# GpSimd multiplies the mask into the fourth head group of each attention chunk, VectorE into the first three

## The reference, cut to what matters

```python
w = softmax(einsum('btc,fc->btf', x, w_lin).reshape(B, T, 16, 31))
kidx = s_idx - t_idx + 30                      # place of source s among the taps of token t
we = where((kidx >= 0) & (kidx < 31), take_along_axis(w, clip(kidx, 0, 30)), 0)
out = einsum('bhts,bhsr->bhtr', we, xh)        # 16 channels a head
x = x + layernorm(out)
```

## Time and profile before

| | |
|---|---|
| median of 3 runs | 1038.87 us (1035.18 to 1041.07) |
| the profiled execution | 1037.57 us, of which the span is 1035.8 us |
| busy over the span | PE 92%, PEld 80%, DVE 82%, ACT 53%, POOL 56% |
| products of half 0 (first `am` to last `residual`) | 93.6 to 196.2 us |
| products of half 1 | 272.9 to 377.3 us |

### The profile page before, as it was taken

The page is one execution under the profiler, slowest core; times in us unless marked ns, Lnnn a source line. Parts: engine busy times, 40 slices in busy tenths (PEclk is TensorE's granted clock), DMA queues, the critical chain, the costliest instruction groups (busy, mean ns, idle before and its releaser), DMA issues.

```text
span 1035.8 us, 26916 instructions
## 1 busy us (share of the span) xinstructions
PE 951.2 (92%) x9256; PEld 833.6 (80%) x9256; DVE 844.7 (82%) x2278; ACT 550.8 (53%) x1308; POOL 582.2 (56%) x843
## 2 busy tenths in 40 slices
PE   5997899899789976899999999999999999999994
PEld 4766788687678865788888899999999878788883
DVE  5887998789799868888886588888888678788886
ACT  4995354799434453333434555555555445454542
POOL 4441655622056540268884366666662688888874
PEclk9998999899999988999999999999999999999996
DMA  5532578843268851122232465555556656665653
GB/s 164 172 110 59 163 208 247 259 124 113 65 173 225 236 186 62 50 88 62 76 119 62 88 202 176 179 177 175 176 180 134 188 178 186 190 199 172 207 166 110
DMA packets 155811, 158.17 MB, mean 153 GB/s; under 512 B 52528, under 2 KB 135600, under 8 KB 155696
## 3 DMA queue, kind: packets, MB, share of 16 engines
q1 hardware_dynamic: 137648, 113.98, 35.7%
q0 software_dynamic: 13056, 35.67, 13.0%
q10 hardware_dynamic: 4992, 6.95, 2.2%
HBM read 91.90 MB, written 64.63 MB: 151 GB/s over the span
## 4 chain that ended last, share of the span: by engine, by line
PE 25%; POOL 17%; DVE 12%; issue 4%; ACT 2%; DMA 1%; POOLq 0%; DVEq 0%; SPq 0%; ACTq 0%
POOL cy L1380 14%; PE bank L1245 11%; PE bank L1261 5%; PE bank L788 3%; PE bank L1230 3%; DVE in_blk L1067 2%; POOL crstd L1389 2%; PE bank L804 2%; DVE in_blk L1066 2%; DVE hf L768 2%; DVE hl L774 2%; ACT hh L751 1%; PE bank L1254 1%; DVE el L1074 1%; POOL crstd L1387 1%
## 5 line engine op out<-in xcount | busy, mean ns | idle before, releaser
L843 POOL DMA_INDIRECT xg<-yn_scratch,ids x144 | 137.0, 951 | 94.2 <-PE bank L1230 65.3
L1380 POOL DMA_INDIRECT cy<-expert_rows,slots x128 | 143.4, 1120 | 56.4 <-issue 36.5
L751 ACT ACTIVATE hh<-hf 128x512 fp32r<-128x512 f32 x96 | 60.7, 633 | 202.9 <-DVE hf L768 202.9
L788 PE MATMUL bank<-yh,gh 128*128 128x512 f32 x352 | 141.0, 401 | 12.5 <-DVE hf L768 12.3
L667 PE MATMUL bank<-xbd,am 128*32 128x68 f32 x4096 | 138.3, 304 | 13.6 <-DMA xbd<-xn_scratch 7.9
L667 PEld LDWEIGHTS bank<-xbd,am 128*32 128x32 f32 x4096 | 123.0, 129 | 21.3 <-issue 10.4
L788 PE MATMUL bank<-yh,gl 128*128 128x512 f32 x352 | 140.1, 398 | 0.0
L788 PE MATMUL bank<-yl,gh 128*128 128x512 f32 x352 | 139.2, 395 | 0.0
L945 POOL TENSOR_SCALAR in_row<-col,row_f 128x128 bf16<-128x128 bf16 x128 | 96.6, 771 | 65.6 <-DVE row_f L1051 39.6
L804 PE MATMUL bank<-dh,hh 128*128 128x256 f32 x384 | 110.2, 292 | 11.8 <-DVE hl L774 8.0
L804 PE MATMUL bank<-dl,hh 128*128 128x256 f32 x384 | 106.5, 282 | 0.0
(11 more groups left out here) (184 smaller groups left out, 2684.2 us busy)
## 6 DMA issues: line engine op xcount, KB each, us to landing
expert_rows<-yo SPq DMA_DIRECT2D x144, 128.0 KB
xbd<-xn_scratch SPq DMA_DIRECT2D x128, 72.0 KB, 2.3
xt<-xp SPq DMA_DIRECT2D x32, 256.0 KB, 2.7
xn_scratch<-xn SPq DMA_DIRECT2D x64, 128.0 KB, 2.7
xr<-x SPq DMA_DIRECT2D x32, 256.0 KB, 3.6
x_scratch<-x SPq DMA_DIRECT2D x32, 256.0 KB, 3.8
yn_scratch<-yn SPq DMA_DIRECT2D x32, 256.0 KB, 3.7
ynt_scratch<-ynt SPq DMA_DIRECT2D x32, 256.0 KB, 4.4
```

The lines of the kernel that those rows point to most:

```text
L751: self.nc.scalar.activation(self.hh[0:f, g], self.hf[0:f, k], ACT.Copy).then_inc(self.s["hh_ok"], 1)
L788: ins = self.nc.tensor.matmul(self.pb[2 * k + half][:], w[:, c, col:col + P], y[:, n % 2, c, :], start=(j == 0), stop=(j == 5))
L843: return nc.gpsimd.indirect_dma_start(out=to, out_offset=None, in_=yn_d.rearrange("n p c -> (n p) c"), in_offset=bass.IndirectOffsetOnAxis ...
L1380: nc.gpsimd.indirect_dma_start(out=y[:, r, t, j], out_offset=None, in_=yg_d, in_offset=bass.IndirectOffsetOnAxis(ap=slots[:, 2 * unit + t, ...
```

## The change

The fourth product of each chunk (group 3) moves from VectorE to GpSimd, as `masked_last`. In GpSimd's list of step i it stands behind `scales23(i-1)` and makes group 3 of chunk i+1. It has its own semaphore `am3_ok`; TensorE waits for that ahead of group 3 of each half, and ScalarE's `keep` waits for both at the start of the second half. Shapes, operands and values stay as they are.

```diff
+            def masked_last(n):
+                h, i, q = n // NCH, n % NCH, n % 2
+                if i == 0:
+                    po.wait_ge(s["probs_ok"], (h + 1) * J)
+                po.wait_ge(s["pso_full"], n + 1)
+                nc.gpsimd.tensor_tensor(
+                    am[:, q, NG - 1], probs[:, bass.ds(i * CB, CB), NG - 1, None, :].to_broadcast([P, CB, 2, J]),
+                    mask[:, None].to_broadcast([P, CB, 2, J]), ALU.mult).then_inc(s["am3_ok"], 1)
...
                 if 0 <= i - 1 < NCH + 2:
                     scales23(h, i - 1)
+                at(h, i + 1, masked_last)
...
                 ve.wait_ge(s["pso_full"], n + 1)
-                for g in range(NG):
+                for g in range(NG - 1):
                     nc.vector.tensor_tensor(
...
                 if n == NPR:
-                    act.wait_ge(s["am_ok"], NCH * NG)
+                    act.wait_ge(s["am_ok"], NCH * (NG - 1))
+                    act.wait_ge(s["am3_ok"], NCH)
...
                 for g in range(NG):
-                    pe.wait_ge(s["am_ok"], n * NG + g + 1)
+                    if g < NG - 1:
+                        pe.wait_ge(s["am_ok"], n * (NG - 1) + g + 1)
+                    else:
+                        pe.wait_ge(s["am3_ok"], n + 1)
```

More of the change, by code:

```diff
@@ L214, in attention @@
             psx_full xth_ok xtl_ok psl_full mx_ok sub_ok exp_ok pse_full probs_ok
-            xs_in0 xs_in1 am_ok pso_full rs_ok av_ok st2_ok mv2_ok var2_ok dev2_ok norm2_ok
+            xs_in0 xs_in1 am_ok am3_ok pso_full rs_ok av_ok st2_ok mv2_ok var2_ok dev2_ok norm2_ok
             z_ok xr_in0 xr_in1 x2_ok st3_ok mv3_ok yn_ok psy_full ynt_ok psg_full lg_ok
```

## The result

The changed kernel takes 1058.37 us (median of 4 runs, 1056.34 to 1060.02), the kernel before beside it 1039.97 us: ratio 1.0172, 95% interval 1.0146 to 1.0198. It is 18 us slower. The forecast had the direction, its range held the time, but the 9 us that it forecast are half of what came.

What follows compares the result with a forecast made beforehand. The prediction took the ring of GpSimd and ScalarE, 5.80 us a step, as the bound. Steps 6, ramps 4, less 1 back gave +9 us on 1037.57, 1046.6; with 1.3 to the median 1047.9, forecast 1048 us, 80% range 1040 to 1060.

Steps and rivals of the forecast that it cites:

- The ring through GpSimd and ScalarE: Steady steps: residual, scales23 (L361), centred and normal2 wait on each other without gaps and set the step of 5.80 us.
- Rival (d): Steady steps: VectorE is the bound and is relieved, 14.6 us less, 1024 us; chance under 1%, counted with (b).
- (a): Steady steps: TensorE's 1.6 us wait fits into its slack, hidden, no change, 1041 us; chance 21%.
- (b): Steady steps: VectorE's products slip behind L361, which falls from 0.55 to 0.20 us; faster, 1032 us; chance 6%.
- GpSimd's product: Behind L361 in GpSimd's list: the moved product takes 1.29 us, between 0.61 and 2.58, and fits into 2.34 us idle.
- Rival (c): GpSimd's product: repeated operands make it 2.58 us, 23 us in the steps and 6 for ramps, 1067 us; chance 18%.
- lighter form: Of the dear-product rival: half of its loss, or the stores of yn joining the loop, about 1057 us; no separate chance.
- the router loop: Late group 3 delays TensorE, router, put_logits and centred, then the product three chunks on: 0.6 us in two chunks, 0.3 each.
- 0.25 us a chunk, bounds 0.05 and 0.7: Steady steps: the loss taken for TensorE's wait for group 3, over 24 chunks 6 us (1 to 17).
- second loop: Late TensorE delays VectorE's group; GpSimd's product takes the port, moments up to 1.2 us late against 0.4 of slack.
- The ramps: First chunks of each half: later products cost 2 us for each ramp (0.7 to 4), so 4 us.
- What comes back: Places where the ring loses time to transfers: a slower pipeline leaves these more time, 1 us back in all.

## Why the prediction was wrong in size

*What bounds the kernel: right.* The ring through GpSimd and ScalarE sets 5.80 us; without any fourth product it stays 5.80, and with L361 free of the port it is 5.63. Rival (d), VectorE as the bound, fell with the run that leaves the product out: 5 us where it asked for about 15. Rivals (a), no change, and (b), faster, fell with the measured time and with TensorE's wait.

*GpSimd's product: right,* 1.25 to 1.30 us by itself, in an idle place of its list. Rival (c), a dear product, fell too. Its lighter form named 1057 us, close to the measured 1058, but for causes that the trace doesn't have: the product isn't dear, and ScalarE's waits name a store of yn once in both halves, for 2.0 us in half 1. It is also by this form that the range reached up to 1060.

*TensorE waits and the router loop: the mechanism right, and its 12.2 us right to 0.1,* as the run with the third product behind the moments shows. TensorE's wait was to be over 1 us in most steps; it is 0.97 us in one step and 0.27 in the next.

*The step that failed is the term "0.25 us a chunk, bounds 0.05 and 0.7".* The forecast named a second loop, in which TensorE's lateness delays VectorE's group and the port then makes the moments late, and counted it among "other waits can add"; for the sum it took less than even the router loop's 0.3, on the ground that products sliding behind L361 give time back. That second loop sets the pace. Read from the timeline above it closes: from the end of one L379 to TensorE's end of the chunk 3.4 us, VectorE's group 3.0, division and moments 2.4, `scales23` 2.2, the next L379 1.7, together 12.7 us for two chunks. An undisturbed step is 0.54 us longer, inside the bounds and twice the value taken. Over the 22 steps from chunk 2 to 13 the loss is 8.9 us, 0.40 a step, where 6 less 1 were forecast. Opening that loop in three ways (another order on TensorE, a third buffer, another order on VectorE) brought the undisturbed step from 6.34 us to 5.79, 5.82 and 6.10: all, all and about half of the 0.54.

*The ramps: mis-sized,* 3.6 us each instead of 2, as the run with the ramps on VectorE shows. The forecast's own bound of 0.7 to 4 us held it. Group 3 of chunk 2 was as late as worked out (it ends at 107.8, forecast 107.7), but what this starts was left out: the same second loop, with VectorE's group of 4.02 us. With TensorE's order changed a ramp cost 1.8 us, near the 2 of the forecast.

*What comes back: open.* Before, four steps from chunk 2 to 13 were over 5.80 us by 0.1 us or more, by 3.9 us together (6.65 in half 0; 5.95, 7.64 and 6.83 in half 1); after, one is longer than the others, 7.97 against 6.34, by 1.6 us. That is 2 us back where 1 was allowed. But such steps also vary by this much among the kernels with a step of 5.80 us (2 to 4 us together), so no run shows it apart.

*Of what the profile was to show:* the group of 32, the waits of TensorE and the longer step came; VectorE's busy time did not fall by 20 us, because its waits for the port are part of its instructions, and the rest of the program kept its length within its scatter.

## What to carry to other kernels

Before moving work to an idle engine, find when the consumer wants the result and what the new owner does ahead of it: here the work fitted into idle time, and TensorE still waited 0.97 us for it in every second step, because it stood behind a chain that VectorE's list hadn't had ahead of it. Then close every loop that the late result starts, over as many chunks as there are buffers, and let the longest one set the step; naming the second loop as a remark and taking a value below the first is how much of the loss was missed, in the steps and in the ramps. Work that reads SBUF on GpSimd should not be placed where a late VectorE can slide onto it.

## What the runs showed of the hardware

Repeated operands cost GpSimd nothing: 1.25 us for the 128x512 product against 1.29 for a plain one. At the port the waiting engine gets its turn at the next end of an instruction: in groups of products that follow one another without a gap, GpSimd's product came in after one of them and the next took 1.8 instead of 0.68 us (three products 3.01 instead of 1.86). Such a wait is counted as busy time of the waiting instruction on either engine (GpSimd's product 1.75 instead of 1.25 us), so VectorE's 42.3 busy us of 48 hide it. Fills on GpSimd of the same length left VectorE's products at 677 ns. After a wait of 2.21 us TensorE's granted clock was at its lower level, 0.50 of full speed, from 161.4 to 162.6 us, and four transposes took 1.11 instead of 0.66 us.
